# Self-attention of a decoder: zeros from GpSimd instead of a mask matmul on TensorE

## The reference

```python
q = (x @ Wq)...; k = (x @ Wk)...; v = (x @ Wv)...    # 16 query heads, 4 key heads, 16 wide; rotary
att = jnp.einsum('bhqd,bhkd->bhqk', q, k) * scale
causal = jnp.tril(jnp.ones((seq_len, seq_len), dtype=bool))
att = jnp.where(causal, att, jnp.finfo(att.dtype).min)
att = jax.nn.softmax(att, axis=-1)
y = jnp.einsum('bhqk,bhkd->bhqd', att, v)
```

## Time and profile before

| | us |
|---|---|
| median of 3 runs | 1419.32 (1416.87 to 1419.46) |
| profiled execution: its own time | 1423.18 |
| its span | 1421.3 |
| PE busy | 1218.8 (86%) |
| PEld busy | 801.9 (56%) |
| DVE busy | 709.6 (50%) |
| ACT busy | 528.7 (37%) |
| POOL busy | 485.6 (34%) |

### The profile page before, as it was taken

The page is one execution under the profiler, slowest core; times in us unless marked ns, Lnnn a source line. Parts: engine busy times, 40 slices in busy tenths (PEclk is TensorE's granted clock), DMA queues, the critical chain, the costliest instruction groups (busy, mean ns, idle before and its releaser), DMA issues. The chain is left out here.

```text
span 1421.3 us, 22346 instructions
## 1 busy us (share of the span) xinstructions
PE 1218.8 (86%) x6643; PEld 801.9 (56%) x6684; DVE 709.6 (50%) x1924; ACT 528.7 (37%) x995; POOL 485.6 (34%) x924
## 2 busy tenths in 40 slices
PE   7689898999869859999999999995988577999990
PEld 3244444444344458767667676784555445778760
DVE  4666666677165426122222222295776425434755
ACT  1257677777656513132222223332333101222210
POOL 6333333121432320122222222113232376806846
PEclk9589999999989958999999999997998577999995
DMA  3970000000000044201010101124200023656743
GB/s 133 331 275 2 1 0 1 0 0 1 1 1 1 1 155 206 74 27 34 31 38 31 38 31 36 50 87 168 87 1 0 19 96 115 215 156 191 213 124 102
DMA packets 64406, 109.20 MB, mean 77 GB/s; under 512 B 7345, under 2 KB 52658, under 8 KB 61362
## 3 DMA queue, kind: packets, MB, share of 16 engines
q1 hardware_dynamic: 54418, 80.96, 16.4%
q0 software_dynamic: 9888, 27.01, 5.9%
HBM read 65.61 MB, written 42.34 MB: 76 GB/s over the span
## 5 line engine op out<-in xcount | busy, mean ns | idle before, releaser
L1390 ACT ACTIVATE f_work<-f_bank,f_ub 128x128 f32<-128x128 f32 x312 | 84.8, 382 | 241.6 <-DVE f_work L1516 221.9
L494 ACT ACTIVATE att_PT<-att_ST 128x1024 f32<-128x1024 f32 (+1 forms) x192 | 148.1, 808 | 66.3 <-PE att_ST L608 34.8
L527 DVE CUSTOM_DVE_ANT_0 att_junk<-att_RB,att_causal_q 128x128 f32<-128x128 f32 (+3 forms) x256 | 120.9, 487 | 60.2 <-PE att_RB L590 48.2
L590 PE MATMUL att_RB<-att_kT,att_qT 96*128 96x512 bf16 (+3 forms) x384 | 122.0, 358 | 23.2 <-DVE att_mx L527 7.2
L1698 PE MATMUL f_bank<-wd_down,f_work 128*128 x624 | 141.2, 380 | 0.5 <-ACT f_work L1390 0.5
L1678 PE MATMUL f_bank<-wu_up,f_work 128*128 x312 | 140.5, 593 | 0.7 <-DVE f_work L1502 0.7
L1698 PEld LDWEIGHTS f_bank<-wd_down,f_work 128*128 128x128 f32 x624 | 115.7, 191 | 14.6 <-issue 0.7
L1339 POOL DMA_INDIRECT Yd<-f_work,f_inv x39 | 38.5, 988 | 236.5 <-DVE f_work L1516 236.5
L1508 DVE COPY f_work<-f_bank 128x512 f32<-128x512 f32 x78 | 54.0, 692 | 120.3 <-PE f_bank L1678 120.3
L2753 PE MATMUL f_bank<-w_w,f_xT 128*128 x376 | 95.5, 398 | 7.8 <-DVE f_xT L2602 3.7
L590 PEld LDWEIGHTS att_RB<-att_kT,att_qT 96*128 96x128 bf16 x384 | 33.9, 99 | 115.5 <-issue 39.8
(11 more groups left out here) (456 smaller groups left out, 2345.3 us busy)
## 6 DMA issues: line engine op xcount, KB each, us to landing
Xd<-g_zero SPq DMA_DIRECT2D x1, 12032.0 KB, 38.2
f_xin<-Xd SPq DMA_DIRECT2D x47, 256.0 KB
Yd<-f_yo SPq DMA_DIRECT2D x47, 256.0 KB
wu_up<-up_w SPq DMA_DIRECT2D x9, 1024.0 KB, 14.4
wd_down<-down_w SPq DMA_DIRECT2D x9, 1024.0 KB, 18.3
w_w<-w SPq DMA_DIRECT2D x6, 768.0 KB, 10.0
wu_up<-Yd SPq DMA_DIRECT2D x16, 256.0 KB, 6.1
w_w<-w SPq DMA_DIRECT2D x1, 2304.0 KB, 18.0
```

The source lines that it names most:

```text
L494: act.activation(buf[:, :, 0:w], ST[:, 2 * (k % 2):2 * (k % 2) + 2, 0:w], ACT.Exp, scale=float(HD) ** -0.5).then_inc(exp_done, 1)
L527: dve.tensor_tensor_reduce(junk[:, k % RING, 0:w], RB[:, bank, 0:w], G.causal_q[:, 512 - w:512], 1.0, LOWEST, ALU.add, ALU.max, to).then_i ...
L590: pe.matmul(RB[:, bank, 0:w], qT[1 - p][0:MROW, r, t * P:(t + 1) * P], kT[1 - p][0:MROW, 512 * c:512 * c + w], start=True, stop=True).then ...
L1390: last = act.activation(hT[:, m, :], bank[:, TB_ + m // 4, (m % 4) * P:(m % 4 + 1) * P], ACT.Gelu, bias=ub[:, ds(e, 1), m])
```

## The change

GpSimd gets a function `pick`, which for each of units 16 to 23 waits for the exponential and then writes zeros above the diagonal, in place: an `affine_select` over the first 128 columns of both heads, 128 x 256 floats. "pv" of these units waits for `picked` instead of `exp_done`. PE leaves out the mask matmuls of these units and keeps those of units 0 to 7. The selects of units 16 and 17 stand ahead of `negate_max` of head 2 in GpSimd's order, those of 18 to 23 ahead of that of head 3. Iteration 7 has no negations; its eight selects stand ahead of `X.constants(pool)`.

```diff
+    PICKED = NU - 8
...
+            def pick(i, units):
+                for k in units:
+                    pool.wait_ge(exp_done, NU * i + k + 1 + EXP_CREDIT)
+                    settle(pool, G.passed)
+                    part = PT[k % 4][:, :, 0:P]
+                    pool.affine_select(out=part, in_=part, compare_op=ALU.is_ge, fill=0.0, base=0,
+                                       pattern=[[0, 2], [1, P]], channel_multiplier=-1).then_inc(picked, 1)
...
                 for r in range(REP):
+                    if r == 2:
+                        pick(i, range(PICKED, PICKED + 2))
+                    if r == 3:
+                        pick(i, range(PICKED + 2, NU))
                     negate_max(i + 1, 1 - p, r)
...
             step(6, 0, False)
+            pick(7, range(PICKED, NU))
             X.constants(pool)
...
-                        diag = kt >= 4 * c
+                        diag = kt >= 4 * c and c == 0
...
-                        pe.wait_ge(exp_done, NU * i + k + 1 + EXP_CREDIT)
+                        if k >= PICKED:
+                            pe.wait_ge(picked, (NU - PICKED) * i + k - PICKED + 1)
+                        else:
+                            pe.wait_ge(exp_done, NU * i + k + 1 + EXP_CREDIT)
```

More of the change, by code:

```diff
@@ L361, in attention_stage @@
     st_ready, exp_done, pv_done = sem("st_ready"), sem("exp_done"), sem("pv_done")
-    ot_copied = sem("ot_copied")
+    ot_copied, picked = sem("ot_copied"), sem("picked")
+    PICKED = NU - 8
     pool_chain, dve_chain = sem("pool_chain"), sem("dve_chain")
```

## The result

The changed kernel takes 1431.63 us (median of 6 runs, 1429.35 to 1433.18) against 1421.35 for the kernel before (6 runs, 1416.87 to 1426.1): ratio 1.0078, 95% interval 1.006 to 1.0095, that is 8.5 to 13.5 us more. Timed once more on another chip, beside the experiments, it was 1.0053 (1.0039 to 1.0067), 5.5 to 9.5 us more. It is slower, by less than 1%, and the forecast of +13.0 us (1432.3) lies at the upper edge of the first interval and above the second.

The account below looks back on a forecast made before the run. PE (86% busy) looked like the bound, with the seam's end set by a chain through GpSimd. Seven iterations x 0 plus 13.0 us for the set-up, on the 1419.32 us median, made 1432.3 us; range 1427.5 to 1437.0.

Parts of the forecast that it names:

- The set-up: End of attention: next stage's set-up starts only after iteration 7's last select, takes 15.26 us, delaying next stage 13.0 us.
- Rival 3: Stage end: the set-up stays covered beside the new stage and the masks' 7.1 us are won, 1412.2 us; chance 0.03.
- The masks: PE in the attention loop: 128 mask matmuls removed at 0.055 us each, 0.89 us an iteration, 7.1 us in all.
- g: Seam between iterations: time by which exponentials 22 and 23 end earlier; 0 to 0.80 us, taken as 0.45 to 0.5.
- The selects in the loop: GpSimd in the loop: 0.55 us a select, fourth negation 0.47 us late, iteration gains 0 us, bounds -0.5 and +0.35.
- a wait at unit 19: PE ahead of P times V: waiting for pick 19 loses some 0.4 us of the 0.67 us gained until there.
- a chain through GpSimd: Seam between iterations: DVE's last row maximum, GpSimd's five small steps (279.18 to 281.11), then the transpose at 281.31 set its end.
- This other chain: Seam between iterations: exponentials, P times V, copy, output transpose, trm; called close to the GpSimd chain, no size given.
- Iteration 6: Iteration without K transpose as cover: output copy starts behind pick 23, a loss of 0.5 - g, about 0 us.
- my own signs: Wrong if next stage starts before 392 us or loop changes over 3.5 us; also selects 0.50 us, copy distances within 0.5.
- Rival 1: Loop: selects never hold PE up (pitch near 0.3 us), iterations 0 to 6 gain 0.89 each; +6.8 us, 1426.1; chance 0.15.
- rival 4: Next stage's start: PE at 1.2 GHz throughout its first groups, 3.2 us more, 1435.5 us; chance 0.08.

## Why the prediction was right, and what in it was not

*The set-up.* Right in place, length and price: 15.27 us for 15.26 foreseen, start of the next stage 15.1 us behind the last copy, and a common start of all engines. Holding back the set-up alone shows it (+12.6 us by time, +12.9 by trace, for 13.0). Rival 3, that it stays covered by other work, is refuted by the same run.

*The masks.* 0.055 us each was right: without them iterations 3 and 5 are 0.85 us shorter (0.89 foreseen), though 1 and 6 only 0.69 and 0.67. (Sixteen of them make 0.88 us, not the 0.80 that I set as the upper bound of g.)

*The selects in the loop: this step failed.* It said: pitch 0.55 us, negation 0.47 us late, iteration gains g - 0.47, in all nothing. It took g as 0.45 to 0.5, after 0.4 us lost in a wait at unit 19. Measured: the select of 128 x 256 takes 0.41 us, and 0.36 in a row, below the lower bound of 0.47. The row it was taken from, L723, has a pattern with one dimension more and another comparison, and still takes 503 ns; which of the two makes it slower was not tried. This is the group in the profile after (in the order of rows 3):

```profile
L440 POOL TENSOR_SCALAR_AFFINE_SELECT att_PT<-att_PT 128x256 f32<-128x256 f32 x64 | 25.4, 408 | 99.3 <-ACT att_PT L509 98.4
```

And this is the seam after, that answers to the earlier trace rows:

```profile
272.08 0.66 ACT L509 ACTIVATE att_PT<-att_ST 128x256 f32<-128x256 f32 x2
...
272.63 0.77 POOL L440 TENSOR_SCALAR_AFFINE_SELECT att_PT<-att_PT 128x256 f32<-128x256 f32 x2 [2.20 <-ACT att_PT L509]
...
273.37 0.24 POOL L428 TENSOR_SCALAR att_negm<-att_rowmax 128x8 f32<-128x8 f32 x1
...
274.97 0.24 POOL L432 TENSOR_TENSOR att_qst<-att_rest_m,att_qst 128x8 bf16<-128x8 f32 x1 [0.18 <-POOL att_qst L431]
275.26 0.45 PEld L579 LDWEIGHTS att_RB<-g_ident_b,att_qst 128*32 128x32 bf16 x8 [0.28 <-POOL att_qst L432]
```

The exponentials end at 272.74 and the negation starts 0.63 us later, not 0.90; before it started 0.43 us behind them. So the negation is 0.2 us late and not 0.47, and the transpose comes 2.52 us behind the exponentials, where it was 2.56. That late start costs nothing, because the chain through GpSimd had room that I had not seen. Before, it ended 0.20 us ahead of the transpose in this iteration, and 0.28 ahead in the one before, where nothing on GpSimd releases the transpose:

```profile
239.30 0.66 PE L626 MATMUL att_RB<-g_ident_f,att_oT 128*128 128x128 f32 x4 [0.67 <-ACT att_oT L500]
239.36 0.24 POOL L431 TENSOR_TENSOR att_qst<-att_rest_m,att_qst 128x8 bf16<-128x8 f32 x1 [0.18 <-POOL att_qst L430]
239.88 0.45 PEld L564 LDWEIGHTS att_RB<-g_ident_b,att_qst 128*32 128x32 bf16 x8 [0.17 <-issue]
```

So my reading that the seam's end "is set by a chain through GpSimd" was wrong for the kernel before: the releaser named in the earlier trace rows was not what came last. The transpose stood right behind PE's transposes of the output (L626 ends 0.08 us behind its start), and those wait for ACT's copy. This other chain, which I had called close, set the end; with the masks gone it gets shorter, and only then does the chain through GpSimd come last. Against the kernel without masks the selects do cost something: 37.95 us against 37.79 and 37.78 in iterations 3 and 5, so some 0.16 us an iteration where I had 0.87 (0.4 at unit 19 and 0.47 at the seam). Of the 0.68 us that iteration 3 gains against before, 0.04 lie in the seam, so g was 0.64; reckoned the same way it is 0.67 without any select. The loss of 0.4 us at unit 19 did not happen. The mechanism itself is real: wide selects bring it about.

*Iteration 6.* Foreseen about 0, measured +0.12: the selects cost 0.67 (masks kept), the missing masks give most of it back.

*The sum.* Set-up +12.7; masks less selects -0.65 in each of iterations 1, 3 and 5, -0.97 in 2 and 4 (40.13 and 40.27 against 41.11 and 41.23 with the masks and no fall of the clock), +0.1 in 6, 0 in 7, together -3.8; the clock that did not fall -2.3; ahead of the first output copies -1.3, of which 0.8 already ahead of iteration 0's first copy (95.20 against 94.41), before any select. That is +5.3, the trace's own. What belongs to the change is 12.7 - 3.8, less up to 0.5 in iteration 0: 8.4 to 8.9 us. The intervals of both timed results reach it (8.5 to 13.5, 5.5 to 9.5). The forecast was 4 us too high, by the failed step, and in its range because the sure term was by far the larger. That the first median (1431.63) came within 1 us of 1432.3 is luck: 1419.32 and 8.4 to 8.9 make 1427.7 to 1428.2, just inside the lower end of the range, and the second chip's 1426.50 lies outside it. By my own signs I was wrong, too: the next stage starts at 391.33, before 392; the loop's part of the change, 3.8 us, is beyond 3.5 (6.1 with the clock); the distances moved by 0.63 us and more, not within 0.5; and a select lasts 0.41 us, not 0.50. Rival 1, to which I gave 0.15, had the loop's sign and most of its size (-3.8 to -4.3 of -6.2), for a pitch near the one it names.

*The clock after the pause* (rival 4). Before, the first normalisation on GpSimd stood 8.05 us behind the gather (386.04 to 394.09, L875); after, 8.35 us (391.33 to 399.68, L893):

```profile
391.00:401.00 10.00, 8.17 (x40) 6.80 (x40) 5.17 (x15) 5.54 (x14) 3.22 (x5) 0.73 0.00 1
...
399.68 0.23 POOL L893 TENSOR_SCALAR xa_rstd<-xa_mv 128x2 f32<-128x2 f32 x1 [4.18 <-DVE xa_mv L1022]
```

A longer pause cost 0.3 us more at the restart, not 3.2: the short pause already ended at the lower clock. The Trainium skill's rule ("TensorE: Matmul & The Clock Gate", Why this matters for your kernels), that an idle gap between bursts of matmuls brings the lower clock back, agrees with the trace as to the kind (0.73 in this row) and adds next to nothing here.

*Open:* the set-up's place costs 14.3 us by time and 12.7 by trace. The six runs of either kernel lie 5 to 6 us apart, mostly by what comes behind attention (1027.8 to 1036.1 us from the gather to the end in ten profiles, 1036.1 and 1029.3 in the two of the changed kernel), so the rest may be chance. Why the clock falls at the turn of the loop in some executions was not tried; it fell in none to three of the three places, with masks and without.

## What to carry to other kernels

An engine with 30% of busy time (12.31 of 40 us) is not free: ask at each place what is queued behind the new instruction, above all at the end of a stage, where work for the next one may be using the cover that the new wait takes away. Put what waits for late data behind what doesn't; here one exchanged line turned +11.1 and +7.5 us into -5.1 and -6.5. And take the duration of an operation from a row with its own access pattern, or treat the nearest row as no more than a bound on either side.

## What the runs showed of the hardware

An affine select on GpSimd of 128 x 256 floats takes 408 ns over a pattern of two dimensions and 503 ns in L741 (three dimensions), and one of 128 x 512 takes 621 ns, in a row 0.57: doubling the size adds 0.21 us. At the turn of a hardware loop DVE stands still for 2.71 to 3.11 us with no releaser in the profile, in all ten profiles, with and without selects; an iteration behind a turn is 2.0 to 2.6 us longer than one within a trip even where the clock stays up (40.13 against 38.08, 41.11 against 38.71 and 41.23 against 38.63 us). A stretch of the lower clock there adds 0.7 to 1.9 us at the first turn (40.87 and 41.98 against 40.13, 42.54 against 41.11); at the second, 0.2 us in the profile of before, which is not clear of the turn's own scatter.
